# An edge loop on one core: VectorE's messages ahead of its ranks and one-hot rows, ScalarE's tanh behind layer 1's silu

## The chip, the core and the metric

The kernel runs on one core of a Trainium2 chip. The metric is the device time of one execution in microseconds (us), from the first instruction to the last. The kernel before takes 6022.33 us, the median of three runs (6012.38 to 6031.83).

## The reference, cut to what matters

100,000 edges (`src`, `dst`, a weight) join 6,250 nodes of 256 features. The part that the change touches is the message of each edge:

```python
rbf = jnp.exp(-0.5 * ((d[:, None] - centers) / (jnp.abs(widths) + EPS_W)) ** 2)
r = rbf * env[:, None]
r = _silu(r @ rbf_w1 + rbf_b1) @ rbf_w2 + rbf_b2
W = _silu(r @ filt_w1 + filt_b1)
W = _silu(W @ filt_w2 + filt_b2) @ filt_w3 + filt_b3
msg = (x[col] @ node_w + node_b) * W
agg = jax.ops.segment_sum(msg, row, num_segments=x.shape[0])
```

After it come a layer norm with a gate, a second pass of sums over the same edges in both directions, and a last layer norm.

## The kernel before, in words

The program has one stream of instructions per engine, written out by hand, and the streams meet only at counting semaphores. It has three stages: a start (histograms of the nodes, the product `x @ node_w` into the DRAM tensor `y_rows`), the edge loop, and a rest (sums by node, gates, norms, the second pass) which the change leaves alone.

The **edge loop** takes 784 tiles of 128 edges in 196 groups of four (`G0`, `GT`). The bodies are `pe_group` (L994), `act_group` (L672), `dve_group` (L1380) and `exchange` (L541, on GpSimd); `loop` (L326) writes out the first four and last four groups and makes a hardware loop of four groups for those between. For one group g:

- SyncE (`load_de`, L408) loads the distances and the envelope into `de`, a ring of four, once VectorE has made the radial rows of four groups earlier (`rbf_done`).
- ScalarE (`radial`, L625) makes a square and a tanh into `th`, a ring of two. VectorE (`radial_basis`, L1359) makes from it add, reciprocal and multiply, which gives `rbf[b % 2]`.
- TensorE does layer 1 (L961), ScalarE `silu1` (L637), TensorE layers 2 and 3 in one (L967), ScalarE `silu2` (L642), TensorE layer 4 (L978), ScalarE `silu3` in two halves (L649), TensorE layer 5 (L989) in two halves onto a bias that ScalarE writes first (`bias_in`, L664).
- VectorE (`messages`, L1371) multiplies the gathered rows by layer 5's two banks: two instructions, and the next group's bias may be written over each bank after it.
- Each edge also needs its place in an order by node. VectorE makes one-hot rows of the blocks (`one_hot_rank`, L1315, eight instructions), TensorE adds them up (`rank_step`, L938 to L952), VectorE multiplies (`product`, L1324) and reduces (`ranked`, L1331).
- GpSimd writes the four tiles of messages to DRAM by four indirect DMAs (`scatter`, L529), which wait for both instructions of `messages`, and gathers four tiles of `y_rows` for group g + 4 (`gather`, L520).

Within an engine the order of the body is what counts, since a waiting instruction holds back all behind it. The engines work on different groups at a time. TensorE's body for g is layer 4 of g, layers 2 and 3 of g + 1, the rank sums and layer 1 of g + 2, layer 5 of g - 1. ScalarE's and VectorE's bodies are what the change reorders:

```python
act_group: silu3(g, 0) bias_in(g - 1) silu3(g, 1) silu2(g + 1) radial(g + 3) silu1(g + 2) stage_idx(g + 4) stage_rec(g + 1)
dve_group: product(g + 2) ranked(g + 2) one_hot_rank(g + 3) radial_basis(g + 3) messages(g - 1, both halves)
```

`messages(g - 1)` waits for `l5_mm`, the last thing of TensorE's body for g; `product(g + 2)` waits for `rank_mm` of the same body.

Of the kernel before, what the change touches and what calls it, by code (L numbers as in the profile page):

```python
# [50 lines left out]
def build(nc, x, xT, src, dst, wgt, wrow, cols, rows, ln_gb, w1, w2T, f1, f2, f3, node_w, gate_w, out):  # L51
# [10 lines left out]
    with ExitStack() as ctx:  # L62
# [3 lines left out]
        def sem(name):  # L66
            return ctx.enter_context(nc.semaphore(name))
# [191 lines left out]
        squared, tanh_done, rbf_done, rbf_chain = sem("squared"), sem("tanh_done"), sem("rbf_done"), sem("rbf_chain")  # L259
# [52 lines left out]
        def fixed(g):  # L312
            return isinstance(g, int)
# [28 lines left out]
        def ahead(g, k):  # L342
            return not fixed(g) or g + k < G0
# [249 lines left out]
        def _(act):  # L593
# [31 lines left out]
            def radial(g, q, b):  # L625
                act.wait_ge(de_in[b], 32 * q + 32)
                if not (fixed(g) and g == 0):
                    act.wait_ge(tanh_done, g)
                if not (fixed(g) and g < 2):
                    act.wait_ge(rbf_done, g - 1)  # L630
                A(sq, de[b][:, 0, :], ACT.Square, bias=negc[:, 0:1]).then_inc(squared, 1)
                act.wait_ge(squared, g + 1)
                A(th[b % 2], sq, ACT.Tanh, scale=zscale[:, 0:1]).then_inc(tanh_done, 1)

            def silu1(g, b):
                act.wait_ge(l1_mm, g + 1)
                A(s1[b % 2], ps[:, 0, 0:GW], ACT.Silu, bias=col[:, 2:3]).then_inc(s1_done, 1)  # L637

            def silu2(g):
                act.wait_ge(l23_mm, g + 1)  # L640
                for m in range(2):
                    A(s2[:, m, :].rearrange("p (h e) -> p h e", h=2),  # L642
                      ps[:, 1:3, m * GW:(m + 1) * GW], ACT.Silu, bias=b23[:, m:m + 1]).then_inc(s2_done, 1)

            def silu3(g, b, m):
                if m == 0 and not (fixed(g) and g < 2):
                    act.wait_ge(l5_mm, 2 * g - 2)
                act.wait_ge(l4_mm, 2 * g + m + 1)
                A(s3[b % 2][:, m, :], ps[:, 3 + m, :], ACT.Silu, bias=col[:, 5 + m:6 + m]).then_inc(s3_done, 1)  # L649

            def stage_idx(g, q, b):
                if not (fixed(g) and g < 4):
                    hold(act, gathered[b], 16 * GT * q)
                A(idx[b][:, :], natrec[:, bass.ds(g * GT, GT), 1], ACT.Copy).then_inc(idx_staged, 1)

            def stage_rec(g, q, b):
                if not (fixed(g) and g < 4):
                    hold(act, scattered[b], 16 * GT * q)
                A(msg[b][:, :, H + 1:H + 5], natrec[:, bass.ds(g * GT, GT), :], ACT.Copy).then_inc(rec_staged, 1)
                act.wait_ge(rank_done, g + 1)  # L660
                A(msg[b][:, :, H + 5], rank8[b % 2][:, :, 1], ACT.Copy).then_inc(rec_staged, 1)
                A(adr[b][:, :], rank8[b % 2][:, :, 0], ACT.Copy).then_inc(rec_staged, 1)

            def bias_in(g):  # L664
                for h in range(2):
                    if fixed(g) and g == 0:
                        act.wait_ge(opened, 1)
                    else:
                        act.wait_ge(msg_done, 2 * g + h - 1)
                    A(ps[:, 5 + h, :], b3[:, :, :].rearrange("p a b -> p (a b)"), ACT.Copy).then_inc(biased, 1)  # L670

            def act_group(g, q, b):  # L672
                silu3(g, b, 0)
                if not (fixed(g) and g == 0):
                    bias_in(g - 1)
                silu3(g, b, 1)
                if ahead(g, 1):
                    silu2(g + 1)
                if ahead(g, 3):
                    radial(g + 3, q + (b + 3) // 4, (b + 3) % 4)  # L680
                if ahead(g, 2):
                    silu1(g + 2, b)
                if ahead(g, 4):
                    stage_idx(g + 4, q + 1, b)
                if ahead(g, 1):
                    stage_rec(g + 1, q + (b + 1) // 4, (b + 1) % 4)
# [5 lines left out]
            for g in range(4):  # L692
                stage_idx(g, 0, g)
            radial(0, 0, 0)
            radial(1, 0, 1)
            silu1(0, 0)
            silu1(1, 1)
# [482 lines left out]
        def _(dve):  # L1180
# [143 lines left out]
            def product(g, b):  # L1324
                dve.wait_ge(rank_mm, g + 1)
                if not (fixed(g) and g == 0):
                    dve.wait_ge(rank_done, g)
                V.tensor_tensor(prod[:, :, :], hot_r[b % 2], ps[:, 7, 0:GT * NB2].rearrange("p (t n) -> p t n", t=GT),  # L1328
                                ALU.mult).then_inc(prod_done, 1)
# [29 lines left out]
            def radial_basis(g, b):  # L1359
                dve.wait_ge(tanh_done, g + 1)  # L1360
                V.tensor_scalar(up1, th[b % 2], 1.0, None, ALU.add).then_inc(rbf_chain, 1)
                dve.wait_ge(rbf_chain, 2 * g + 1)
                if not (fixed(g) and g == 0):
                    dve.wait_ge(rbf_done, g)
                V.reciprocal(rcp, up1).then_inc(rbf_chain, 1)  # L1365
                dve.wait_ge(rbf_chain, 2 * g + 2)
                if not (fixed(g) and g < 2):
                    dve.wait_ge(l1_mm, g - 1)
                V.scalar_tensor_tensor(rbf[b % 2], rcp, -0.5, de[b % 4][:, 1, :], ALU.add, ALU.mult).then_inc(rbf_done, 1)

            def messages(g, q, b, h):  # L1371
                if h == 0:
                    dve.wait_ge(gathered[b], 16 * GT * q + 16 * GT)
                    if not (fixed(g) and g < 4):
                        dve.wait_ge(scattered[b], 16 * GT * q)
                dve.wait_ge(l5_mm, 2 * g + h + 1)
                V.tensor_tensor(msg[b][:, 2 * h:2 * h + 2, 0:H], gath[b][:, 2 * h:2 * h + 2, :],
                                ps[:, 5 + h, :].rearrange("p (a b) -> p a b", a=2), ALU.mult).then_inc(msg_done, 1)

            def dve_group(g, q, b):  # L1380
                if ahead(g, 2):
                    product(g + 2, b)
                    ranked(g + 2, b)
                if ahead(g, 3):
                    one_hot_rank(g + 3, b + 1)
                    radial_basis(g + 3, b + 3)
                if not (fixed(g) and g == 0):
                    for h in range(2):
                        messages(g - 1, q + (b + 3) // 4 - 1, (b + 3) % 4, h)

            for g in range(2):
                one_hot_rank(g, g)
# [3 lines left out]
                product(g, g)  # L1396
                ranked(g, g)
            one_hot_rank(2, 2)
            radial_basis(2, 2)
            loop(dve, dve_group, G0, 4, 4, 4)  # L1400
            for b in range(2):
                dve.wait_ge(y_out[b], 16 * slot_uses(CHUNKS, b))
# [285 lines left out]
```

## Time and profile before

| what | value |
|---|---|
| median of three runs | 6022.33 us (6012.38 to 6031.83) |
| profiled execution | 6008.27 us, its span 6006.5 us |
| TensorE matmul, busy | 3694.8 us (62%) |
| GpSimd, busy | 3415.2 us (57%) |
| VectorE, busy | 2377.6 us (40%) |
| ScalarE, busy | 1607.1 us (27%) |
| mean granted clock of TensorE | 0.781 |

The page's strip of 40 slices shows the stages: up to slice 20 all engines work at steady shares (TensorE 7 tenths, GpSimd 5, VectorE 4, ScalarE 3, clock 8 to 9 tenths). That is the edge loop, some 117 to 2977 us of the span. No engine there is busy all the time, so the time must be read from who waits for whom, in a stretch of the loop. In the rows below "remote" and "issue" are the profile's words for a wait whose releaser it didn't find.

### The profile page before, as it was taken

Reading aid. Unit: us, or ns where it says so; the run is one execution under the profiler, and the core shown is the slowest. Engines: PE = TensorE matmul, PEld = TensorE weight load, DVE = VectorE, ACT = ScalarE, POOL = GpSimd, SP = SyncE. Lnnn points to the kernel's source line nnn. Section 1 sums busy time; section 2 is a strip of 40 time slices with the busy share of each in tenths; the row PEclk is TensorE's granted clock in tenths of the full one; section 3 lists DMA queues with packets and bytes.
Section 4 is the critical chain, followed back from the end, with each engine's and each line's share of the span. In section 5 each row is a group of like instructions: output and inputs, shape, how many; then the busy total and the mean of one; then the engine's idle time right before and its main releaser. Section 6 shows DMA issues by size and latency. Waiting matters only on the chain. (4 is left out here: it accounts for less than half of the span.)

```text
span 6006.5 us, 76202 instructions
## 1 busy us (share of the span) xinstructions
PE 3694.8 (62%) x16356; PEld 2677.7 (45%) x16357; DVE 2377.6 (40%) x7105; ACT 1607.1 (27%) x4212; POOL 3415.2 (57%) x3664
## 2 busy tenths in 40 slices
PE   7777777777777777777799833333332444455444
PEld 5444444444444444444588632222222444444443
DVE  5434434344344443334233622221222445555457
ACT  4333333333333333333366611111111000000000
POOL 2455555554555555555576566666666666566665
PEclk9888888888888888888899966656665667777776
DMA  7333333332333333332499311111111333333334
GB/s 217 94 97 98 95 97 101 95 101 90 94 97 95 95 97 100 98 99 91 131 296 295 120 48 43 44 44 45 44 44 44 99 84 85 84 85 84 84 85 90
DMA packets 460154, 590.18 MB, mean 98 GB/s; under 512 B 65457, under 2 KB 380849, under 8 KB 460081
## 3 DMA queue, kind: packets, MB, share of 16 engines
q0 software_dynamic: 128512, 318.04, 17.5%
q1 hardware_dynamic: 331584, 271.50, 15.6%
q8 instruction: 21, 0.34, 0.0%
q14 instruction: 37, 0.30, 0.0%
HBM read 392.61 MB, written 197.07 MB: 98 GB/s over the span
## 5 line engine op out<-in xcount | busy, mean ns | idle before, releaser
L533 POOL DMA_INDIRECT s_rows<-arena,adr x784 | 770.6, 983 | 1118.4 <-issue 1095.7
L978 PE MATMUL ps<-arena,f2s 128*128 128x512 f32 x1568 | 864.3, 702 | 427.5 <-ACT arena L642 335.3
L573 POOL DMA_INDIRECT d_rows<-arena,adr x832 | 809.5, 973 | 501.1 <-issue 243.6
L586 POOL DMA_INDIRECT arena<-x_half,idx x832 | 800.9, 963 | 507.1 <-issue 230.9
L525 POOL DMA_INDIRECT arena<-y_rows,idx x784 | 758.0, 967 | 305.3 <-issue 227.0
L989 PE MATMUL ps<-f3s,arena 128*128 128x256 f32 x3136 | 800.2, 406 | 171.0 <-issue 112.8
L1166 PE MATMUL ps<-arena 128*128 128x128 f32 x1664 | 376.9, 397 | 649.7 <-DVE arena L1559 566.8
L989 PEld LDWEIGHTS ps<-f3s,arena 128*128 128x128 f32 x3136 | 632.5, 204 | 306.7 <-issue 130.0
L978 PEld LDWEIGHTS ps<-arena,f2s 128*128 128x128 f32 x1568 | 349.8, 229 | 854.1 <-issue 472.1
L1328 DVE TENSOR_TENSOR arena<-arena,ps 128x392 f32<-128x392 bf16 x196 | 109.6, 559 | 1448.1 <-remote 1338.1
L1166 PEld LDWEIGHTS ps<-arena 128*128 128x128 f32 x1664 | 325.6, 292 | 692.7 <-issue 691.5
L1502 DVE TENSOR_TENSOR arena<-rec,ps 128x512 f32<-128x512 f32 x208 | 142.4, 685 | 952.5 <-remote 870.5
L1114 PE MATMUL ps<-agg,arena 128*128 x1664 | 340.2, 367 | 221.1 <-issue 176.8
L649 ACT ACTIVATE arena<-ps,col 128x512 f32<-128x512 f32 x392 | 267.3, 682 | 752.7 <-remote 441.2
L1103 PE MATMUL ps<-ident_b,arena 128*128 128x128 bf16 x832 | 107.8, 271 | 580.2 <-DVE arena L1490 504.0
L642 ACT ACTIVATE arena<-ps,b 128x512 f32<-128x512 f32 x392 | 247.4, 684 | 647.6 <-remote 604.5
L1114 PEld LDWEIGHTS ps<-agg,arena 128*128 128x128 f32 x1664 | 298.3, 268 | 244.2 <-issue 244.1
L782 ACT ACTIVATE arena<-ps 128x512 f32<-128x512 bf16 x208 | 123.7, 595 | 1036.6 <-remote 882.5
L1580 DVE TENSOR_TENSOR arena<-arena,ps 128x129 f32 x832 | 239.5, 288 | 404.1 <-issue 254.7
L1058 PE MATMUL ps<-arena 128*128 128x257 f32 x1664 | 375.3, 385 | 17.7 <-POOL arena L563 11.9
L1058 PEld LDWEIGHTS ps<-arena 128*128 128x128 f32 x1664 | 308.6, 190 | 84.9 <-issue 43.1
L1365 DVE RECIPROCAL arena<-arena 128x256 f32<-128x256 f32 x196 | 343.6, 1753 | 6.8
(217 smaller groups left out, 5073.0 us busy)
## 6 DMA issues: line engine op xcount, KB each, us to landing
arena<-s_rows SPq DMA_DIRECT2D x104, 1048.0 KB, 5.7
arena<-d_rows SPq DMA_DIRECT2D x52, 1040.0 KB
arena<-de_rows SPq DMA_DIRECT2D x392, 128.0 KB
d_rows<-arena,adr POOLq DMA_INDIRECT x832
arena<-x_half,idx POOLq DMA_INDIRECT x832
s_rows<-tpl_s SPq DMA_DIRECT2D x98, 131.0 KB
arena<-y_rows,idx POOLq DMA_INDIRECT x784
s_rows<-arena,adr POOLq DMA_INDIRECT x784
```

What stands on the lines that cost most here:

```text
L525: pool.indirect_dma_start(gath[b][:, t, :], None, y_rows, bass.IndirectOffsetOnAxis(ap=idx[b][:, t:t + 1], axis=0)).then_inc(gathered[b], 16)
L533: pool.indirect_dma_start(s_rows, bass.IndirectOffsetOnAxis(ap=adr[b][:, t:t + 1], axis=0), msg[b][:, t, :], None).then_inc(scattered[b], 16)
L573: pool.indirect_dma_start(d_rows, bass.IndirectOffsetOnAxis(ap=adr2[b][:, t:t + 1], axis=0), drow[b][:, t, :], None).then_inc(scattered_d[ ...
L586: pool.indirect_dma_start(gath2[b][:, t, :], None, x1_half, bass.IndirectOffsetOnAxis(ap=idx2[b][:, t:t + 1], axis=0)).then_inc(gathered2[ ...
L642: A(s2[:, m, :].rearrange("p (h e) -> p h e", h=2), ps[:, 1:3, m * GW:(m + 1) * GW], ACT.Silu, bias=b23[:, m:m + 1]).then_inc(s2_done, 1)
L649: A(s3[b % 2][:, m, :], ps[:, 3 + m, :], ACT.Silu, bias=col[:, 5 + m:6 + m]).then_inc(s3_done, 1)
L978: last = mm(ps[:, 3 + m, :], f2s[:, k, m * P:(m + 1) * P], s2[:, k, :], start=(k == 0), stop=(k == 1))
L989: last = mm(o, s3[b % 2][:, k, t * P:(t + 1) * P], f3s[:, k, :], start=False, stop=False, skip_group_check=True)
L1058: mm(slots[:, bass.ds(at[k * GT + t], H + 1)], hot[(2 * b + k) % 4][:, t, :], s_buf[b][:, k * GT + t, 0:H + 1], start=False, stop=False, s ...
L1114: last = mm(ps[:, spread_bank(g, b), t * P:(t + 1) * P], hot_t[b % 4][:, t * P:(t + 1) * P], agg[:, bass.ds(places[t] + HALF, HALF)], star ...
L1166: mm(forth[:, bass.ds(at[t], HALF)], hot_f[b][:, t, :], gath2[b][:, t, :], start=False, stop=False, skip_group_check=True).then_inc(aggf_m ...
L1365: V.reciprocal(rcp, up1).then_inc(rbf_chain, 1)
```

## The change

VectorE makes the radial rows of g + 2 first (they were those of g + 3), then the messages, then product, ranks and one-hot rows. ScalarE does `silu1(g + 2)` before `radial(g + 3)`. `radial` loses its wait for `rbf_done`, and the radial rows of group 2 are no longer made ahead of the loop.

```diff
@@ radial
                 if not (fixed(g) and g == 0):
                     act.wait_ge(tanh_done, g)
-                if not (fixed(g) and g < 2):
-                    act.wait_ge(rbf_done, g - 1)
                 A(sq, de[b][:, 0, :], ACT.Square, bias=negc[:, 0:1]).then_inc(squared, 1)
@@ act_group
                     silu2(g + 1)
+                if ahead(g, 2):
+                    silu1(g + 2, b)
                 if ahead(g, 3):
                     radial(g + 3, q + (b + 3) // 4, (b + 3) % 4)
-                if ahead(g, 2):
-                    silu1(g + 2, b)
                 if ahead(g, 4):
@@ dve_group
                 if ahead(g, 2):
+                    radial_basis(g + 2, b + 2)
+                if not (fixed(g) and g == 0):
+                    for h in range(2):
+                        messages(g - 1, q + (b + 3) // 4 - 1, (b + 3) % 4, h)
+                if ahead(g, 2):
                     product(g + 2, b)
                     ranked(g + 2, b)
                 if ahead(g, 3):
                     one_hot_rank(g + 3, b + 1)
-                    radial_basis(g + 3, b + 3)
-                if not (fixed(g) and g == 0):
-                    for h in range(2):
-                        messages(g - 1, q + (b + 3) // 4 - 1, (b + 3) % 4, h)
@@ ahead of the loop
             one_hot_rank(2, 2)
-            radial_basis(2, 2)
             loop(dve, dve_group, G0, 4, 4, 4)
```

VectorE, the first group of the loop's body, before. L1328 is `product`, L1335 `ranked`, L1320 `one_hot_rank` (of its eight instructions the first stands here), L1361 to L1369 `radial_basis`, L1377 `messages`; in brackets the semaphores.

```order
L1328 TENSOR_TENSOR arena<-arena,ps 128x392 [waits rank_done]
L1334 ISA [waits prod_done]
L1335 TENSOR_REDUCE rank<-arena 128x8 [waits rec_staged]
L1320 ISA [waits rank_mm]
L1320 TENSOR_SCALAR arena<-lane,arena 128x49
...
L1361 TENSOR_SCALAR arena<-arena 128x256 [waits tanh_done]
L1362 ISA
L1365 RECIPROCAL arena<-arena 128x256 [waits rbf_done,rbf_chain]
...
L1376 ISA [waits scattered3,gathered3]
L1377 TENSOR_TENSOR arena<-arena,ps 128x2x256 [waits l5_mm]
```

The same group after the change, whose lines stand two lower (L1326 is `product`, L1333 `ranked`, L1318 `one_hot_rank`, L1359 to L1367 `radial_basis`, L1375 `messages`).

```order
L1359 TENSOR_SCALAR arena<-arena 128x256 [waits tanh_done]
L1360 ISA
L1363 RECIPROCAL arena<-arena 128x256 [waits rbf_done,rbf_chain]
...
L1367 SCALAR_TENSOR_TENSOR arena<-arena 128x256 [waits l1_mm]
...
L1374 ISA [waits scattered3,gathered3]
L1375 TENSOR_TENSOR arena<-arena,ps 128x2x256 [waits l5_mm]
...
L1326 TENSOR_TENSOR arena<-arena,ps 128x392 [waits rank_done,rank_mm]
L1332 ISA [waits prod_done]
L1333 TENSOR_REDUCE rank<-arena 128x8 [waits rec_staged]
L1318 ISA [waits rank_mm]
L1318 TENSOR_SCALAR arena<-lane,arena 128x49
```

The wait for `l5_mm` now stands ahead of the wait for `rank_mm`, and eleven instructions that stood ahead of the messages stand behind them. The three radial instructions stay between the one-hot rows and the messages that follow.

ScalarE, one group of the loop's body, before and then after. L631 and L633 are `radial`, L637 is `silu1`, L642 `silu2`; after the change L629, L631, L635 and L640.

```order
L642 ACTIVATE arena<-ps,b 128x512 [waits l23_mm]
L642 ACTIVATE arena<-ps,b 128x512
L626 ISA
L631 ACTIVATE arena<-arena,negc 128x256 [waits rbf_done,tanh_done,de_in0]
L632 REGISTER_ALU
L633 ACTIVATE arena<-arena,zscale 128x256 [waits squared]
L637 ACTIVATE arena<-ps,col 128x256 [waits l1_mm]
```

```order
L640 ACTIVATE arena<-ps,b 128x512 [waits l23_mm]
L640 ACTIVATE arena<-ps,b 128x512
L635 ACTIVATE arena<-ps,col 128x256 [waits l1_mm]
L626 ISA
L629 ACTIVATE arena<-arena,negc 128x256 [waits tanh_done,de_in0]
L630 REGISTER_ALU
L631 ACTIVATE arena<-arena,zscale 128x256 [waits squared]
```

The square and the tanh of g + 3 now stand behind the wait for layer 1 of g + 2, and the wait for `rbf_done` is gone.

## Rows read from the trace of the kernel before

**Rows 1.** Stretches: us, each engine's busy us, clock, DMA share, GB/s; the edge loop

```profile
117.00:2977.00 2860.00, 2118.75 (x8142) 1296.01 (x8140) 1146.69 (x2879) 1031.12 (x2512) 1515.23 (x1556) 0.86 0.31 97
```

**Rows 2.** Groups of instructions from 900 to 2900 us: busy, mean ns | idle before

```profile
L533 POOL DMA_INDIRECT s_rows<-arena,adr x544 | 535.0, 984 | 774.1 <-issue 774.1
L525 POOL DMA_INDIRECT arena<-y_rows,idx x544 | 525.6, 966 | 165.8 <-issue 157.9 <-DVE arena L1377 7.9
...
L631 ACT ACTIVATE arena<-arena,negc 128x256 f32<-128x256 f32 x136 | 69.2, 509 | 0.0
L633 ACT ACTIVATE arena<-arena,zscale 128x256 f32<-128x256 f32 x136 | 69.1, 508 | 4.4
```

**Rows 3.** Waits from 900 to 2900 us: us in total, times, longest

```profile
DVE arena L1328 <- remote: 926.5, 57, 17.2
...
ACT arena L642 <- remote: 438.3, 49, 12.9
```

**Rows 4.** Timeline, a long pause of GpSimd: start, us, instruction [idle before]

```profile
2022.77 1.00 POOL L533 DMA_INDIRECT s_rows<-arena,adr  x1 [9.94 <-issue]
...
2030.67 0.33 PE L951 MATMUL ps<-arena,before_b 128*128 128x392 bf16 x1
...
2041.94 0.95 POOL L525 DMA_INDIRECT arena<-y_rows,idx  x1 [0.30 <-issue]
2044.47 1.27 ACT L642 ACTIVATE arena<-ps,b 128x512 f32<-128x512 f32 x2 [9.91 <-remote]
2045.79 6.06 PE L978 MATMUL ps<-arena,f2s 128*128 128x512 f32 x8 [7.10 <-ACT arena L642]
2046.05 0.56 DVE L1328 TENSOR_TENSOR arena<-arena,ps 128x392 f32<-128x392 bf16 x1 [17.20 <-remote]
2050.90 1.28 DVE L1377 TENSOR_TENSOR arena<-arena,ps 128x512 f32<-128x512 f32 x2
2053.20 1.00 POOL L533 DMA_INDIRECT s_rows<-arena,adr  x1 [10.31 <-issue]
```

**Rows 5.** Timeline, the short pause of GpSimd right behind it

```profile
2053.89 0.56 DVE L1328 TENSOR_TENSOR arena<-arena,ps 128x392 f32<-128x392 bf16 x1 [1.71 <-PE ps L951]
2055.07 1.32 DVE L1320 TENSOR_SCALAR arena<-lane,arena 128x49 bf16<-128x49 f32 x8
2055.79 0.98 POOL L533 DMA_INDIRECT s_rows<-arena,adr  x1 [0.30 <-issue]
2062.16 0.95 POOL L525 DMA_INDIRECT arena<-y_rows,idx  x1 [0.30 <-issue]
2065.13 0.69 DVE L1377 TENSOR_TENSOR arena<-arena,ps 128x512 f32<-128x512 f32 x1 [5.70 <-remote]
2065.21 0.69 ACT L649 ACTIVATE arena<-ps,col 128x512 f32<-128x512 f32 x1 [8.95 <-remote]
2066.84 1.00 POOL L533 DMA_INDIRECT s_rows<-arena,adr  x1 [3.73 <-issue]
2067.41 1.26 ACT L642 ACTIVATE arena<-ps,b 128x512 f32<-128x512 f32 x2
```

**Rows 6.** Timeline, TensorE's pieces of one group at full clock, and layer 5 at less

```profile
2054.12 3.62 PE L989 MATMUL ps<-f3s,arena 128*128 128x256 f32 x16
2057.58 3.60 PE L978 MATMUL ps<-arena,f2s 128*128 128x512 f32 x8
2061.10 1.13 PE L967 MATMUL ps<-arena,w 64*128 64x256 f32 x8
...
2063.02 0.59 PE L961 MATMUL ps<-arena,w1d 128*128 128x256 f32 x2
2066.44 5.41 PE L989 MATMUL ps<-f3s,arena 128*128 128x256 f32 x16 [2.83 <-ACT ps L670]
```

**Rows 7.** Stretches as in rows 1, within the long pause

```profile
2046.00:2050.00 4.00, 4.00 (x5) 1.62 (x6) 3.79 (x12) 1.79 (x8) 0.00 (x0) 0.50 0.00 0
```

**Rows 8.** SyncE's queue, waits from 900 to 2900 us

```profile
SPq L413 <- DVE arena L1369: 975.9, 83, 21.5
```

## The prediction

> **What bounds the kernel now.** I read the stretches by stage first. The edge loop takes 2860 us of the 6006.5 us span [rows 1]; that is 2860 / 196 = 14.59 us a group, and the rest of the program isn't touched. TensorE is busy 2119 us of it, GpSimd 1515 us, VectorE 1147 us, ScalarE 1031 us: none is full, so the loop is bound by a cycle of waits.
>
> The groups of instructions show GpSimd's part of that cycle. A group costs it eight indirect DMAs of about 0.97 us with 0.30 us between them. Its first scatter of a group starts at 2053.20 and its last gather ends at 2062.16 + 0.95 = 2063.11 [rows 4, 5]: a burst of 9.91 us. Ahead of the scatters it sat idle 774.1 us in 2000 us, of which 544 x 0.30 = 163 us is the fixed spacing [rows 2]. So GpSimd pauses 611 us in the 136 groups of that stretch, 4.5 us a group, and a pause ends when VectorE's two message instructions are done: they end at 2050.90 + 1.28 = 2052.18, the scatter starts 1.02 us later [rows 4].
>
> The waits show why the messages are late. VectorE waits 926.5 us, in 57 waits of up to 17.2 us, at `product` (L1328), with no releaser found [rows 3]. The timeline of one such wait shows what is odd: TensorE's rank sums end at 2031.00 by the record, yet `product` starts at 2046.05, and `silu2` on ScalarE, also fed by TensorE, starts at 2044.47 after 9.91 us [rows 4]. Both start 1.6 to 3.2 us after GpSimd's last gather ended (2041.94 + 0.95 = 2042.89). In the next burst the same happens: layer 5 ends at 2057.74 by the record [rows 6], its second message starts at 2065.13, and `silu3` at 2065.21, 2.0 and 2.1 us after the burst's end at 2063.11 [rows 5]. At the start of a burst it is otherwise: `product` at 2053.89 starts 1.71 us after it began to wait, at once when the rank sums ended [rows 5]. **My reading**: some microseconds into a burst of GpSimd's indirect DMAs TensorE's completions stop getting through, and they come together some 2 us (3 us behind a burst of two groups) after the burst ends. What holds them no row says; that they are held is in every long wait above.
>
> What VectorE does first after this release then sets GpSimd's pause. There are two kinds. In the long pause VectorE stood at `product`: it makes product, ranks, one-hot rows and radial rows (2046.05 to 2050.90, 4.85 us), then the messages, and GpSimd has paused 10.31 us [rows 4]. In the short one VectorE stood at a message, and GpSimd paused 3.73 us [rows 5]. The long kind follows a burst of two groups: 2053.20 - 2022.77 = 30.43 us for two groups, 15.2 us each. The short kind is 2066.84 - 2053.20 = 13.64 us for one group.
>
> **The change part by part.** *VectorE's order.* No instruction is added or removed in the loop. The wait for `l5_mm` now stands first, so every pause is of the short kind: after the release the messages come at once. A group then costs burst 9.91 + release 2.02 + both messages 1.28 + start of the scatter 1.02 = 14.23 us; where layer 5's first half came through ahead of the release, as in rows 5, one message less is left and it is the measured 13.64 us. I take 13.8 us, nearer to the measured short cycle, since all its parts are in one row pair.
>
> What was ahead of the messages is late next: 4.85 us of work now starts 1.28 us after the release, and TensorE waits for it. The one-hot and radial rows are done 1.28 + 4.85 = 6.13 us after the messages start. TensorE then has layer 1 (0.59 us) and layer 5 (3.62 us, or 5.41 us at a lower clock) [rows 6], so the next layer 5 is complete after 10.3 to 12.1 us. The cover is GpSimd's own cycle of 13.8 us; if that were gone, this chain would be the bound at 10.4 to 12.2 us. So it costs nothing, by 1.7 us or more.
>
> *ScalarE's order.* `silu1` waits for layer 1 and now holds back square and tanh, 1.02 us [rows 2]. If layer 1 is released only with everything else, tanh is ready 0.5 + 1.0 = 1.5 us after the release, while VectorE reaches the radial rows only after messages, product, ranks and one-hot rows: 1.28 + 0.56 + 0.56 + 1.32 = 3.7 us. Cost nothing; without that cover at most 1.5 us a group. Queued behind the wait are `stage_idx` and `stage_rec`, whose users (GpSimd's next burst) are a whole cycle away. The dropped wait for `rbf_done` is implied by the wait for layer 1: nothing.
>
> *SyncE.* `load_de` waits for `rbf_done`, which now comes one group later; the queue waits long for it already [rows 8], since it runs four groups ahead. It keeps three groups, over 40 us. Nothing, and the radial rows of group 2, moved from ahead of the loop into it, are one set of three instructions: nothing.
>
> *VectorE beside GpSimd.* The one-hot rows now fall into every burst, where they fell into the pause in the long cycles. The row says that this is free: with one-hot rows at 2055.07 to 2056.39 the scatter at 2055.79 took 0.98 us, as the mean does (0.984) [rows 2, 5]. The Trainium skill ("SBUF — State Buffer", Who interferes with whom) says that `tensor_scalar` on VectorE can take a port pair that it shares with GpSimd, and that GpSimd is then blocked for the whole instruction and can't write the descriptors of its DMAs. By that rule the one-hot rows' 1.32 us would be added to a burst in the 57 of 136 groups that gain them, 196 x 57 / 136 x 1.32 = 108 us.
>
> **The sum.** 196 x (14.59 - 13.8) = 155 us less: 6008 - 155 = 5853 us for the profiled execution. The median of the runs is 14 us above that execution; I say 5855 us. By the ends 13.64 and 14.23 us it is 6008 - 186 = 5822 and 6008 - 71 = 5937 us.
>
> **The rivals.**
>
> *Two-group bursts stay, with the short pause.* If layer 5 often gets through before the burst ends, GpSimd runs two groups on end: 30.43 - 4.85 = 25.6 us for two, 12.8 us each, 6008 - 196 x 1.8 = 5657 us. For it: 57 long waits in 136 groups are bursts that did this. Against: those rested on TensorE having one-hot and radial rows ready, and the next layer 5 now comes 8.1 us into the burst (10.3 less 1.28 and 1.02), when completions are mostly held.
>
> *Slower: the pause was what TensorE and ScalarE lived on.* In the long pause layer 4 ran at once after the release and before the new burst; now the burst starts 2.3 us after the release (1.28 + 1.02), and what TensorE finishes later than some 4 us into it is held to the next release (the half of layer 5 that ended 4.5 us into the burst was, at 2057.74). If ScalarE then stands at `silu3`, it must do both halves, the bias and `silu2` first: 2065.21 to 2068.67, 3.5 us [rows 5]. TensorE goes on with layer 4 (6.06 us at the clock of 0.50 that the pause left [rows 4, 7]), layers 2 and 3 (1.13), rank sums (0.8), layer 1 (0.6) and layer 5 (5.41): 17.5 us a group, 6008 + 196 x 2.9 = 6576 us. It decides from the point at which this chain is over the 13.8 us; at full clock it is 3.5 + 3.6 + 1.1 + 0.8 + 0.6 + 3.6 = 13.2 us, so it hangs on the clock and on where ScalarE stands. Against: after one such slow cycle layer 5 ends when nothing is held, ScalarE runs ahead, and the next cycle is a fast one. A third of such cycles gives (2 x 13.8 + 17.5) / 3 = 15.03 us, 6008 + 86 = 6094 us.
>
> *No change*: a few slow cycles among fast ones, 14.6 us a group.
>
> *The port rule*: GpSimd's bursts grow by the one-hot rows. By the row it would be 0; with 1.32 us for each of those groups it is 5853 + 108 = 5961 us, still faster.
>
> *That it does nothing at all* I leave out: the listing shows the wait for `l5_mm` ahead of that for `rank_mm`.
>
> **How the numbers follow.** What a measurement of this kernel can tell from no change is about 0.3%, 18 us. Forecast (13.6 to 14.3 us a group, 5815 to 5955 us) 0.52, the port rule with it 0.05; two-group bursts, wholly or in part (5650 to 5815 us) 0.17; no change 0.08; slower by slow cycles 0.18. So faster 0.74, same 0.08, slower 0.18. The range takes the first three and no change: 5660 to 6020 us; below lies a little of the second case, above nearly all of the slow one.
>
> **What would show it.** Right: the waits of VectorE at `product` nearly vanish and stand at the messages; GpSimd's pauses of 10 us are gone and pauses of some 4 us follow each burst; the loop ends near 2820 us of the span; scatters keep 0.98 us each. Wrong: pauses of 7 us and more ahead of scatters with TensorE at work in them (the slow chain), a clock below 0.86 in the loop, bursts longer than 9.9 us (the port), or messages that wait although GpSimd has stopped.

## The result, and the profile after

The changed kernel takes 5721.7 us (median of 4 runs, 5719.0 to 5722.5) where the kernel before takes 6017.4 us (4 runs, 6007.9 to 6031.8): a ratio of 0.951, with an interval of 0.949 to 0.953. That is faster, and inside the range of 5660 to 6020 us; but the gain is 296 us where the forecast had about 160.

Two stretches of the changed kernel's profile, the edge loop and the rest (columns as in [rows 1]), and two lines of its page, the span and the busy times:

```profile
117.00:2687.00 2570.00, 2108.01 (x8144) 1347.30 (x8142) 1161.60 (x2891) 1032.67 (x2513) 1533.95 (x1556) 0.89 0.36 108
2680.00:5720.00 3040.00, 1481.39 (x7790) 1310.39 (x7790) 1159.81 (x4033) 525.58 (x1603) 1882.33 (x2081) 0.71 0.33 94
```

```profile
span 5720.7 us, 76061 instructions
...
PE 3678.5 (64%) x16356; PEld 2722.4 (48%) x16357; DVE 2387.8 (42%) x7105; ACT 1607.6 (28%) x4212; POOL 3435.5 (60%) x3664
```

The loop took 2860 us [rows 1] and takes 2570 us, 290 us less, with the same busy times to within some 20 us. A group costs 2570 / 196 = 13.11 us. TensorE is busy 64% of the span, no engine is full. Behind the loop both kernels need the same: 6006.5 - 2977 = 3030 us before, 5720.7 - 2687 = 3034 us now. So all of the gain is in the loop's waits.

The groups of instructions of the changed kernel from 900 to 2900 us, of which the loop has the part up to 2687 (busy, mean ns | idle before); they answer to [rows 2]:

```profile
L533 POOL DMA_INDIRECT s_rows<-arena,adr x546 | 550.3, 1008 | 552.6 <-issue 522.0 <-ACT adr L660 17.5 <-DVE arena L1375 7.0
...
L1375 DVE TENSOR_TENSOR arena<-arena,ps 128x512 f32<-128x512 f32 x272 | 185.9, 689 | 938.8 <-remote 440.8 <-issue 268.4 <-PE ps L987 229.5
...
L1326 DVE TENSOR_TENSOR arena<-arena,ps 128x392 f32<-128x392 bf16 x133 | 73.9, 555 | 0.0
```

GpSimd's idle time ahead of the scatters, less 0.30 us each, is 552.6 - 546 x 0.30 = 389 us in 136.5 groups: 2.85 us a group where it was 4.5. That is 1.65 us less; 0.10 us of it goes back into longer scatters (1008 ns, before 984, four a group), and 1.55 us is left, against 290 / 196 = 1.48 us by the loop's length. `product` (L1326) no longer waits at all. VectorE now waits at the messages (L1375), and so does ScalarE at `silu3`. The waits of the same kernel from 900 to 2700 us (us in total, times, longest), beside [rows 3]:

```profile
ACT arena L647 <- PE ps L976: 566.0, 120, 6.3
POOL s_rows L533 <- issue: 522.0, 538, 6.0
DVE arena L1375 <- remote: 440.8, 103, 9.7
...
PE ps L942 <- DVE arena L1318: 126.0, 75, 3.1
```

The longest wait of VectorE was 17.2 us and is 9.7; GpSimd's longest pause was over 10 us and is 6.0. The last line is the price: TensorE now waits for the one-hot rows (L1318), 126 us in all, for which it hardly waited before (9.7 us from 900 to 2900 us).

One cycle in the timeline (start, us, instruction [idle before]), beside [rows 4, 5]:

```profile
2057.79 0.95 POOL L525 DMA_INDIRECT arena<-y_rows,idx  x1 [0.30 <-issue]
...
2060.52 1.29 DVE L1375 TENSOR_TENSOR arena<-arena,ps 128x512 f32<-128x512 f32 x2 [7.73 <-remote]
...
2062.82 1.00 POOL L533 DMA_INDIRECT s_rows<-arena,adr  x1 [4.08 <-issue]
2062.89 1.32 DVE L1318 TENSOR_SCALAR arena<-lane,arena 128x49 bf16<-128x49 f32 x8
...
2064.12 1.15 POOL L533 DMA_INDIRECT s_rows<-arena,adr  x1 [0.30 <-issue]
...
2064.27 0.34 PE L942 MATMUL ps<-arena,after_b 128*128 128x392 bf16 x1 [1.52 <-DVE arena L1318]
...
2067.53 5.02 PE L987 MATMUL ps<-f3s,arena 128*128 128x256 f32 x16
2070.86 0.69 DVE L1375 TENSOR_TENSOR arena<-arena,ps 128x512 f32<-128x512 f32 x1 [4.20 <-issue]
2071.95 0.95 POOL L525 DMA_INDIRECT arena<-y_rows,idx  x1 [0.30 <-issue]
2074.37 0.69 DVE L1375 TENSOR_TENSOR arena<-arena,ps 128x512 f32<-128x512 f32 x1 [2.81 <-remote]
...
2076.08 1.00 POOL L533 DMA_INDIRECT s_rows<-arena,adr  x1 [3.18 <-issue]
```

From scatter to scatter it is 2076.08 - 2062.82 = 13.26 us. The burst takes 2072.90 - 2062.82 = 10.08, the release 2074.37 - 2072.90 = 1.47, one message 0.69, the scatter's start 1.02. Layer 5 ends at 2072.55 by the record, just ahead of the burst's end, and its second message comes only after it: this burst stays one of one group.

One cycle need not be a typical one, so here are all bursts that begin between 900 and 2650 us, counted in the traces (a burst ends where the first scatter of a group waits over 0.6 us; the time is from one burst's start to the next's):

| kernel | bursts of one group | of two groups |
|---|---|---|
| before | 15, mean 13.35 us | 52, mean 29.90 us |
| changed | 116, mean 13.16 us | 8, mean 27.36 us |

Bursts of two groups cost 14.95 us a group in the kernel before and nearly all of its groups lay in them. That they became rare is the bulk of the gain: with bursts of one group alone the kernel before would stand at 13.35 us a group instead of 14.75 by this count, 1.40 of the 1.5 us. The cycle of one group itself became only 0.19 us shorter.

### The profile page after: what moved, and what is told of

Same layout as the page of the kernel before. It is cut to its first block and busy times, and to the rows that moved or that the text cites. A ratio compares the mean times of both kernels' runs of the same rounds, so it can differ in the third digit from the quotient of the medians.

```text
span 5720.7 us, 76061 instructions
## 1 busy us (share of the span) xinstructions
PE 3678.5 (64%) x16356; PEld 2722.4 (48%) x16357; DVE 2387.8 (42%) x7105; ACT 1607.6 (28%) x4212; POOL 3435.5 (60%) x3664
## 5 line engine op out<-in xcount | busy, mean ns | idle before, releaser
L533 POOL DMA_INDIRECT s_rows<-arena,adr x784 | 790.0, 1008 | 809.5 <-issue 765.9
L987 PE MATMUL ps<-f3s,arena 128*128 128x256 f32 x3136 | 878.2, 442 | 40.5 <-issue 40.4
L1375 DVE TENSOR_TENSOR arena<-arena,ps 128x512 f32<-128x512 f32 x392 | 268.0, 689 | 1354.0 <-remote 611.7
L987 PEld LDWEIGHTS ps<-f3s,arena 128*128 128x128 f32 x3136 | 720.7, 230 | 185.3 <-issue 47.9
L976 PE MATMUL ps<-arena,f2s 128*128 128x512 f32 x1568 | 732.2, 611 | 30.9 <-ACT arena L640 29.2
L976 PEld LDWEIGHTS ps<-arena,f2s 128*128 128x128 f32 x1568 | 306.8, 197 | 345.6 <-issue 298.6
L1101 PEld LDWEIGHTS ps<-ident_b,arena 128*128 128x128 bf16 x832 | 77.2, 123 | 587.0 <-DVE arena L1488 496.8
L831 ACT ACTIVATE agg<-ps,rdeg 128x128 f32<-128x128 f32 x49 | 17.8, 367 | 1177.7 <-PE ps L1164 592.3
```

The costliest lines, as they stand in the source:

```text
L533: pool.indirect_dma_start(s_rows, bass.IndirectOffsetOnAxis(ap=adr[b][:, t:t + 1], axis=0), msg[b][:, t, :], None).then_inc(scattered[b], 16)
L976: last = mm(ps[:, 3 + m, :], f2s[:, k, m * P:(m + 1) * P], s2[:, k, :], start=(k == 0), stop=(k == 1))
L987: last = mm(o, s3[b % 2][:, k, t * P:(t + 1) * P], f3s[:, k, :], start=False, stop=False, skip_group_check=True)
```

## The experiments

They ran in four sittings, each beside the kernel before on the same chip, on chips that the record numbers 7, 0, 9 and 0. The kernel before took 5945, 4688, 4688 and 5992 us in them. Ratios are within a sitting. The result itself is a fifth occasion.

**First sitting (before 5945.3 us, 13 runs): which half of the change?** VectorE's order alone, ScalarE's as before:

```diff
@@ ScalarE, as in the kernel before
+                if not (fixed(g) and g < 2):
+                    act.wait_ge(rbf_done, g - 1)
...
+                if ahead(g, 3):
+                    radial(g + 3, q + (b + 3) // 4, (b + 3) % 4)
                 if ahead(g, 2):
                     silu1(g + 2, b)
-                if ahead(g, 3):
-                    radial(g + 3, q + (b + 3) // 4, (b + 3) % 4)
```

> VectorE's new order alone, ScalarE as before (radial ahead of silu1, with its wait for rbf_done). Theory A (the whole gain is that the messages come first after a release, so GpSimd's pause is short): about the changed kernel's 5722 us, within 20 us. Theory B (the gain needs ScalarE's layer 1 silu early, so that TensorE's layers 2 and 3 run ahead of the held stretch): less than half of the gain, 5880 us or more.

Measured: 5650.3 us, ratio 0.950 (0.947 to 0.952). The time isn't within 20 us of 5722, since the kernel before is faster here as well (5945 us); the ratio is that of the whole change. And the other half alone, VectorE's order as before and ScalarE's as after:

```diff
@@ dve_group, as in the kernel before
                 if ahead(g, 2):
-                    radial_basis(g + 2, b + 2)
-                if not (fixed(g) and g == 0):
-                    for h in range(2):
-                        messages(g - 1, q + (b + 3) // 4 - 1, (b + 3) % 4, h)
-                if ahead(g, 2):
                     product(g + 2, b)
                     ranked(g + 2, b)
                 if ahead(g, 3):
                     one_hot_rank(g + 3, b + 1)
+                    radial_basis(g + 3, b + 3)
+                if not (fixed(g) and g == 0):
+                    for h in range(2):
+                        messages(g - 1, q + (b + 3) // 4 - 1, (b + 3) % 4, h)
```

> ScalarE's new order and the dropped wait alone, VectorE as before. Theory A: no gain, 6000 to 6030 us, with VectorE's waits of 16 to 17 us at product still there. Theory B: half of the gain or more, 5870 us or less.

Measured: 5934.6 us, ratio 0.998 (0.997 to 1.000). VectorE's order is the whole gain, ScalarE's next to nothing, as the prediction costed it. Counted as above, VectorE's half has 103 bursts of one group and 14 of two (and two that break off within a group), ScalarE's half 14 and 54, like the kernel before. The waits of ScalarE's half alone from 900 to 1900 us, with `product` (L1326) as in [rows 3]:

```profile
DVE arena L1326 <- remote: 459.0, 33, 16.6
POOL s_rows L533 <- issue: 384.1, 275, 10.1
```

and of VectorE's half alone in the same stretch:

```profile
POOL s_rows L533 <- issue: 288.9, 307, 5.4
DVE arena L1377 <- remote: 221.8, 46, 9.4
```

**Is it GpSimd's burst that holds TensorE's completions?** If so, short bursts should set them free. Three of the four gathers of a group are left out from the fifth group on, in the changed kernel:

```diff
-                for t in range(GT):
+                for t in range(GT if fixed(g) and g < 4 else 1):
...
-                    hold(act, gathered[b], 16 * GT * q)
+                    hold(act, gathered[b], 16 * q + 16 * GT - 16)
...
-                    dve.wait_ge(gathered[b], 16 * GT * q + 16 * GT)
+                    dve.wait_ge(gathered[b], 16 * q + 16 * GT)
```

> The changed kernel with one of the four gathers of y_rows in each group from the fifth on (the other three tiles of messages are made from old rows): GpSimd's burst falls from 8 to 5 indirect DMAs, 10.0 to 6.2 us. Theory H (TensorE's completions are held while GpSimd issues indirect DMAs and let go some 2 us after the last one): the releases still come 1.6 to 3 us after the now earlier end of the burst, and a group takes what TensorE's own chain takes, 10.5 to 11.5 us against 13.1 now, some 300 to 500 us less in all. Theory T (the pauses are TensorE's and ScalarE's own chain, GpSimd only waits for it): 12.6 us or more a group, under 100 us less.

and, by the same three lines, in the kernel before:

> The same cut of three of the four gathers in the kernel before. Theory H: the waits of VectorE at product fall from 16 to 17 us to under 8 us, since bursts of two groups no longer form or last 12 us at most, and the order of VectorE matters much less: the distance to the changed kernel with the same cut is under 100 us of the 296 us. Theory T: the long waits stay at 14 us or more and the distance stays over 200 us.

Measured: 5043.2 us and 4953.3 us (one run each), with bursts of 6.3 and 6.1 us. The expectation for the first, 10.5 to 11.5 us a group, was too high: it is 9.8. The waits of the changed kernel with one gather, from 900 to 1900 us:

```profile
POOL s_rows L533 <- DVE arena L1375: 361.0, 102, 3.8
...
DVE arena L1375 <- PE ps L987: 290.6, 170, 3.5
```

and of the kernel before with one gather:

```profile
POOL s_rows L533 <- DVE arena L1377: 340.4, 107, 3.9
DVE arena L1328 <- PE ps L951: 188.4, 63, 3.8
```

`product` waits 3.8 us at most, where it waited 17.2: no burst of two groups forms, and the long waits go with them. The same two kernels have 102 and 107 groups in 1000 us, 9.8 and 9.3 us a group. So **the sign turns**: with short bursts the old order is the faster one, by 0.46 us a group, 90 us in all. A distance under 100 us was expected, but not its sign. In the changed kernel a chain through VectorE sets the pace: the second message, then product, ranks, one-hot and radial rows (L1367 is the last of these), layer 1 (L959), layer 5 (L987), the second message again.

```profile
1503.82 0.69 DVE L1375 TENSOR_TENSOR arena<-arena,ps 128x512 f32<-128x512 f32 x1 [0.19 <-PE ps L987]
...
1505.50 0.99 POOL L533 DMA_INDIRECT s_rows<-arena,adr  x1 [3.48 <-DVE arena L1375]
...
1505.59 1.32 DVE L1318 TENSOR_SCALAR arena<-lane,arena 128x49 bf16<-128x49 f32 x8
...
1508.93 0.43 DVE L1367 SCALAR_TENSOR_TENSOR arena<-arena 128x256 f32<-128x256 f32 x1
...
1509.41 0.70 PE L959 MATMUL ps<-arena,w1d 128*128 128x256 f32 x2 [0.18 <-issue]
...
1509.95 3.62 PE L987 MATMUL ps<-f3s,arena 128*128 128x256 f32 x16
```

The next second message starts at 1513.60, 9.78 us after this one. In the kernel before with one gather TensorE itself has no gap: from layer 4 at 1499.52 to layer 4 at 1508.84 it is 9.32 us.

Are TensorE's completions free with such short bursts? The waits above have releasers by name, which suggests it, but the timeline of the kernel before with one gather says no:

```profile
1505.39 3.62 PE L989 MATMUL ps<-f3s,arena 128*128 128x256 f32 x16
...
1508.54 0.99 POOL L525 DMA_INDIRECT arena<-y_rows,idx  x1 [0.30 <-issue]
...
1510.59 1.29 DVE L1377 TENSOR_TENSOR arena<-arena,ps 128x512 f32<-128x512 f32 x2 [0.22 <-remote]
1510.76 0.69 ACT L649 ACTIVATE arena<-ps,col 128x512 f32<-128x512 f32 x1 [3.58 <-PE ps L978]
```

The burst began at 1503.39. Layer 5 ends at 1509.01 by the record, 0.5 us before the burst's end at 1509.53, and the messages start at 1510.59. From 900 to 1900 us all 68 message instructions that had to wait were of this kind: their half of layer 5 ended inside the burst and they started 0.90 to 1.15 us after its end. So a burst of 6.1 us holds completions too, by up to 3.7 us; it is only that little hangs on them here. In the changed kernel with one gather layer 5 ends after the burst, and most messages start 0.04 us later.

The rest of the program (5041.3 and 4951.3 us of span, less 117 us and the loops of 1917 and 1830 us) took 3007 and 3004 us, nearly as ever: it was the loop's burst that changed, not the state of the chip.

**Second sitting (before 4687.5 us, 31 runs): variants of the new order.** Four kernels: the ranks behind the one-hot rows; scatters that start behind the first message; product and ranks ahead of the messages; and the changed kernel again as the yardstick.

```diff
@@ ranks last
                 if ahead(g, 2):
                     product(g + 2, b)
-                    ranked(g + 2, b)
                 if ahead(g, 3):
                     one_hot_rank(g + 3, b + 1)
+                if ahead(g, 2):
+                    ranked(g + 2, b)
@@ split scatter
-                hold(pool, msg_done, 2 * g + 2)
+                hold(pool, msg_done, 2 * g + 1)
...
+                    if t == 2:
+                        hold(pool, msg_done, 2 * g + 2)
@@ product first
                 if ahead(g, 2):
                     radial_basis(g + 2, b + 2)
+                    product(g + 2, b)
+                    ranked(g + 2, b)
                 if not (fixed(g) and g == 0):
                     for h in range(2):
                         messages(g - 1, q + (b + 3) // 4 - 1, (b + 3) % 4, h)
-                if ahead(g, 2):
-                    product(g + 2, b)
-                    ranked(g + 2, b)
```

> The changed kernel with ranked behind the one-hot rows, so that TensorE's rank sums, which wait for the one-hot rows (285 us of waits in 1800 us), can start 0.56 us earlier. If TensorE's chain is hidden under GpSimd's burst, as the prediction has it: within 20 us of the changed kernel. If TensorE's chain sets part of the cycles (the rival that the pause was what TensorE lived on): 40 us or more faster.

> The changed kernel with GpSimd scattering the two tiles of the first message instruction before it waits for the second. Theory A alone (only the path from the first message to the scatter counts): 0.6 us or more off every pause, 100 to 200 us faster than the changed kernel. Theory H (a running burst holds TensorE's completions): where the scatters of the first half start before layer 5's second half is complete, that completion is held and GpSimd stands in the middle of a burst; the gain is under 50 us, or it is slower.

> The changed kernel with product and ranks (1.24 us of the 4.85 us) ahead of the messages again, one-hot rows behind. Theory A (each microsecond that VectorE does between a release and the messages lengthens GpSimd's pause and is paid): 1.2 us in most groups, 0.7 to 1.2 us x 196 = 140 to 240 us slower than the changed kernel. Theory P (the gain is that product is no longer waited for first, and the work after it is hidden): within 40 us of the changed kernel or back at the kernel before, nothing between.

> The changed kernel again, as the mark for the runs beside it: 0.951 of the kernel before, as on the first chip.

Measured: 4680.2 us (0.9985, interval 0.9975 to 0.9994), 4685.2 (0.9995), 4685.6 (0.9995) and, for the changed kernel itself, 4685.1 us: 0.9993 (0.9983 to 1.0002). The 0.951 expected of the changed kernel did not come: **the change is worth nothing in this sitting**, and the kernel before takes 22% less time in it than in the result. The three variants lie within 5 us of the changed kernel. Some of the forecasts ("within 20 us", "within 40 us", "under 50 us") allow that, but where the change itself gains nothing it decides between no theories. A stretch of the changed kernel, its loop, and its waits from 900 to 1900 us show why:

```profile
122.00:2119.00 1997.00, 1894.13 (x8064) 1172.79 (x8063) 1158.01 (x2862) 1007.55 (x2493) 1517.13 (x1556) 1.00 0.46 138
```

```profile
DVE arena L1375 <- PE ps L987: 388.2, 196, 3.4
...
POOL s_rows L533 <- issue: 119.5, 392, 0.3
```

GpSimd never pauses: 392 scatters wait 0.30 us each. A group takes 1997 / 196 = 10.19 us, eight indirect DMAs of 0.97 + 0.30 us. The messages come while a burst runs, as the timeline of the same kernel shows:

```profile
1503.74 3.72 PE L987 MATMUL ps<-f3s,arena 128*128 128x256 f32 x16 [0.20 <-ACT ps L668]
...
1505.81 1.00 POOL L533 DMA_INDIRECT s_rows<-arena,adr  x1 [0.30 <-issue]
...
1507.50 0.69 DVE L1375 TENSOR_TENSOR arena<-arena,ps 128x512 f32<-128x512 f32 x1 [1.04 <-PE ps L987]
```

Layer 5 ends at 1507.46 and the second message starts 0.04 us later, in an unbroken run of indirect DMAs; the 196 messages that waited from 900 to 1900 us all started within 0.14 us of their half of layer 5. So TensorE's completions are not held here. GpSimd's and VectorE's instructions take what they take elsewhere: scatters 986 ns (984 in [rows 2]), messages 689 ns. TensorE's granted clock in the loop is 1.00, where it was 0.89 in the result, and it is busy 1894 us instead of 2108. The rest of the program is shorter too, 4679.8 - 2119 = 2561 us against 3034.

**Third sitting (before 4688.0 us, 19 runs).** Two of the variants again, unchanged.

> Product and ranks (1.24 us) ahead of the messages again, a second time, in case this chip holds TensorE's completions as the first two did (the kernel before at 5900 us or more); then theory A says 0.97 to 0.99 of the kernel before against 0.950 for the changed order, theory P within 0.007 of 0.950 or of 1. If the kernel before takes about 4690 us here, the chip doesn't hold them, as the third one did not, and everything is within 0.3% of it.

> Two tiles scattered after the first message instruction, a second time. On a chip that holds completions theory A alone says 0.92 to 0.935 of the kernel before; theory H says 0.945 or more, since the burst that has begun holds the second half of layer 5. On a chip that doesn't: within 0.3% of the kernel before.

Measured: 4684.5 us (0.999, 0.998 to 1.000) and 4682.9 us (0.999, 0.998 to 1.000). The holds are absent again, and both are within 0.3% of the kernel before, as expected for that case; they decide nothing between the theories, and say only that these orders gain nothing where GpSimd runs without pauses.

**Fourth sitting (before 5992.4 us, 7 runs): the holds are back,** on a chip with the same number, 0, as in the second. Product and ranks ahead of the messages once more, 1.24 us in every pause by the prediction's reading:

> Product and ranks (1.24 us) ahead of the messages again, a third time. If the kernel before takes 5900 us or more here (completions held): theory A 0.97 to 0.99 of it, theory P within 0.007 of 0.950 or of 1. If it takes about 4690 us: within 0.3% of it.

Measured: 5713.4 us, ratio 0.952 (0.950 to 0.955), the gain of the whole change (in another sitting) to within 0.002. So **it isn't that product and ranks stand ahead of the messages** that the kernel before pays for. The waits from 900 to 1900 us, and the timeline of one cycle:

```profile
POOL s_rows L533 <- issue: 269.4, 295, 5.4
...
DVE arena L1326 <- remote: 108.7, 12, 12.8
```

```profile
1499.33 1.32 DVE L1318 TENSOR_SCALAR arena<-lane,arena 128x49 bf16<-128x49 f32 x8
...
1500.43 1.00 POOL L533 DMA_INDIRECT s_rows<-arena,adr  x1 [3.55 <-issue]
...
1501.39 0.33 PE L949 MATMUL ps<-arena,before_b 128*128 128x392 bf16 x1
...
1503.02 0.56 DVE L1326 TENSOR_TENSOR arena<-arena,ps 128x392 f32<-128x392 bf16 x1
```

The one-hot rows end at 1500.65, the rank sums at 1501.72, 1.3 us into the burst, and `product` is done 3.2 us into it, long before the pause. So the 1.24 us are not in the pause at all here; the run does not show what they would cost if they were. In [rows 4] the rank sums ended 8.2 us into a burst (2031.00 - 2022.77) and got through only after it. That still happens in this order, but seldom: 12 waits at `product` without a named releaser, of up to 12.8 us, where the kernel before has 29 of up to 17.2 in the same stretch. Counted as above, it has 113 bursts of one group (13.19 us) and 9 of two (27.61 us).

Last, a length between: two gathers of four left out, in the changed kernel, with a burst of 7.5 us.

```diff
-                for t in range(GT):
+                for t in range(GT if fixed(g) and g < 4 else 2):
...
-                    hold(act, gathered[b], 16 * GT * q)
+                    hold(act, gathered[b], 32 * q + 16 * GT - 32)
...
-                    dve.wait_ge(gathered[b], 16 * GT * q + 16 * GT)
+                    dve.wait_ge(gathered[b], 32 * q + 16 * GT)
```

> The changed kernel with two of the four gathers in each group from the fifth on (the other two tiles of messages are made from old rows): a burst of 7.5 us, between the 6.2 us of one gather (9.78 us a group, nothing held to a burst's end) and the 10 us of the full kernel (13.1 us a group). If this chip holds completions: with a hold that begins some 4.5 us into a burst, layer 5 ends about 7 us into it and is let go at 7.5 + 1.7 us, which gives 11 us a group or more. If it doesn't: TensorE's own chain of the changed order, 9.8 us a group, is now longer than GpSimd's 7.7 us, so 0.38 us x 196 = 75 us less than the changed kernel's 4685 us, about 4610 us.

Measured: 5239.7 us (one run). From 900 to 1900 us:

```profile
POOL s_rows L533 <- issue: 388.9, 370, 3.7
DVE arena L1375 <- PE ps L987: 329.1, 95, 5.0
```

That is 370 / 4 = 92.5 groups in 1000 us, 10.8 us a group, a little under what was expected. By burst length the changed kernel takes 9.8, 10.8 and 13.2 us a group for bursts of 6.3, 7.5 and 10.0 us (the last in the result's trace, by its bursts of one group). From 6.3 to 7.5 us a group grows by 1.0 us for 1.2 of burst; from 7.5 to 10.0 by 2.4 for 2.5. At 7.5 us layer 5 ends about 8.0 us after the burst's start, so 0.5 us after its end, and its second message still starts 0.7 us late (0.69 to 0.79 us).

## Why the prediction was right and wrong

**That it gains, and where**: right. The gain is in the loop, in GpSimd's pauses; the waits at `product` are gone; nothing behind the loop moved. The pauses of 10 us are gone, as forecast.

**The range**: it held the result, but not by the forecast itself. 5721.7 us lies outside the forecast's own bounds (5815 to 5955 us, chance 0.52) and within those of the first rival (5650 to 5815 us, chance 0.17), two-group bursts with a short pause. That rival isn't what happened: only 8 of 124 bursts were of two groups, at 27.36 / 2 = 13.7 us a group and not 12.8. The range covered the result in part by luck.

**The cycle of 13.8 us**: too long; it is 13.11. The difference of 0.69 us times 196 is 135 us, the whole of what was missing in the forecast. The short cycle was read from one pair of rows, 13.64 us, and then set higher still, towards 14.23; the 15 such cycles counted in the kernel before average 13.35 us. By terms: the release was taken as 2.02 us after the burst's end; the two cycles shown have 1.78 (2058.74 to 2060.52) and 1.47, and of the 64 messages that began only after the burst in which their half of layer 5 ended (changed kernel, 900 to 1900 us), 49 began over 0.3 us after it, at the median 1.56 us. And both messages were left only sometimes: in the second of the cycles shown one is gone by the time of the release, which with the shorter release gives 13.26.

**"So every pause is of the short kind: after the release the messages come at once."** The outcome was right for 116 of 124 bursts, but the reason given doesn't carry it. The step said that 4.85 us of VectorE's work leaves the pause because the messages are put first. With product and ranks, 1.24 us of it, put back ahead of them the gain stayed whole (0.952 beside 0.951), and a pause of the short kind was as common (113 of 122). What the prediction noted and this step didn't use is that the long pause follows a burst of *two* groups. How such a burst comes about stands in the timeline of the kernel before, from the end of one long pause on:

```profile
2020.13 0.42 DVE L1369 SCALAR_TENSOR_TENSOR arena<-arena 128x256 f32<-128x256 f32 x1
2020.47 1.28 DVE L1377 TENSOR_TENSOR arena<-arena,ps 128x512 f32<-128x512 f32 x2
2020.61 0.70 PE L961 MATMUL ps<-arena,w1d 128*128 128x256 f32 x2 [0.39 <-DVE arena L1369]
...
2021.84 3.72 PE L989 MATMUL ps<-f3s,arena 128*128 128x256 f32 x16 [0.53 <-ACT ps L670]
...
2027.57 1.28 DVE L1377 TENSOR_TENSOR arena<-arena,ps 128x512 f32<-128x512 f32 x2
...
2032.98 1.00 POOL L533 DMA_INDIRECT s_rows<-arena,adr  x1 [0.30 <-issue]
```

The radial rows (L1369) are made in the pause, ahead of the messages, so TensorE has layers 1 and 5 under way before the burst begins at 2022.77 and ends layer 5 at 2025.56, 2.8 us into it, while completions get through. The next messages follow at 2027.57, in the burst, and GpSimd goes on at 2032.98 without a pause. Then the rank sums fall late into it (2031.00), and `product` has to stand until the burst of two groups is over. In every order that gained, the one-hot rows and the next radial rows are made *behind* the messages. Then the rank sums mostly end early in a burst, and layer 5 late:

| kernel, 900 to 2650 us | rank sums that end within 5 us of a burst's start | layer 5 ends, median us after it |
|---|---|---|
| before | 20 of 120 | 5.8 |
| changed | 117 of 132 | 9.7 |
| product first | 106 of 132 | 8.6 |

So bursts mostly stay single, and `product` seldom waits. This reading fits the counts of the changed kernel and of the two orders that gained. It is argued, not shown: no run moves the one-hot and radial rows alone, and no run puts work into the pause itself.

**TensorE's chain, 10.3 to 12.1 us, hidden**: near in size. Laid bare by short bursts it is 9.8 us with the new order. Under a cycle of 13.1 us it is hidden, but the cover depends on the burst: where the burst was 6.3 us, the new order cost 90 us.

**ScalarE, SyncE, the first group**: nothing, as said, for ScalarE (0.998, interval 0.997 to 1.000, for its half). The other two weren't taken apart from VectorE's half, which with them has the whole gain.

**The port rule**: the forecast by the row was 0, by the Trainium skill ("SBUF — State Buffer", Who interferes with whom) 108 us. Measured: the second scatter took 1.15 us at 2064.12 beside the one-hot rows, and the mean scatter grew from 984 to 1008 ns, 0.10 us a group or 19 us in all. Between the two, and far nearer to nothing: the one-hot rows' 1.32 us is not added to the burst. VectorE's half alone has the same growth (1007 ns). With product first (983 ns) the one-hot rows are nearly done when the burst begins, so that run says nothing of it; in the sitting without pauses, where they run beside the DMAs all the time, the mean is 986 ns.

**The slow chain**: it didn't come. Layer 5 took 5.02 us in the cycle shown, as feared (5.41 in [rows 6]), but the loop's granted clock rose from 0.86 [rows 1] to 0.89, and the longest cycle of one group counted is 14.7 us, never 17.5.

**The signs**: the waits at `product`, the pauses of 10 us and the clock came out as forecast. The loop ends at 2687 us and not near 2820, pauses average 3.1 us behind bursts of one group and not some 4, and bursts are 10.04 us on average, above the 9.9 us named as a sign of the port rule.

**What the prediction could not know**: that the whole argument holds only in some sittings. In the second and third "no change" was the case.

## What to carry to other kernels

When an engine seems to be late by what stands ahead of it, put that work back in one experiment, and look in the timeline where it then runs: here 1.24 us put back ahead of the messages cost nothing, because it no longer ran in the pause. Count a pattern over the whole stretch before a forecast rests on one cycle of it: one pair of rows gave 13.64 us where the mean was 13.35. Shorten the thing that is thought to hold the others before you order work around it: a burst of 6.3 instead of 10 us turned the sign of this change, from -290 to +90 us. And compare two kernels within one sitting only, and in more than one: the same kernel took 28% longer in one than in another, and the change was worth 5% or nothing.

## What the runs showed that was not expected

- **TensorE's completions are held during runs of GpSimd's indirect DMAs, on some occasions.** On three of five (6017, 5945 and 5992 us for the kernel before) waits of up to 17.2 us end mostly 1.5 to 3 us after the burst. On two (4688 us) a message starts 0.04 us after layer 5 ends, in the midst of the DMAs. The ends of matmuls are modelled in these traces, but that doesn't explain a wait of 15 us: in the trace of [rows 4] layer 5, which stands behind the rank sums on the same engine, was already under way at 2031.27. And the trace has the semaphores' own times: the rank sums' came at 2045.94, layer 1's at 2045.98, layer 5's at 2046.07 and 2046.16.
- **It isn't a closed door.** In the changed kernel's trace 124 of the messages that waited from 900 to 1900 us had their half of layer 5 end inside a burst, and 51 of them started within 0.2 us of that. What lets some through no row says.
- **The release comes later behind a longer burst**: about 1.0 us after a burst of 6.1 us, 1.2 after 7.5, 1.5 after 10.0 and 2.6 to 3.0 after 20.
- **What holds them isn't shown, and not that it is the chip.** The record gives the second sitting (4688 us) and the fourth (5992 us) the same chip number, 0; if that is one chip, the cause is a state and not the chip. One more thing goes with the holds: in every trace with them a part of the semaphore records is missing (VectorE's in the kernel before: 2961 for 3998 instructions that set one; TensorE's: 2059 for 2304), and in every trace without them none is (4017 and 2313 in the changed kernel of the second sitting). The waits at the messages named "issue" are just those whose record is missing (all 40 in the changed kernel from 900 to 1900 us), while the 59 named "remote" have one that comes late. Whether the recording takes part in the hold stays open.
- The stages behind the loop have it too, or something like it: 3034 us against 2561 us, with the same instructions. They were not looked into.
- Left open: ranks last and the split scatter never ran in a sitting with holds, so whether they add to the gain there isn't known. In the others ranks last was the fastest of all, by 0.1% (4680.2 against 4685.1 us), too little to call it better.
